# Cross attention on one Trainium2 core: weighted sums in five runs per half instead of seven, and a ring of three buffers for the turned probabilities

## The chip, the cores and the metric

One core of one Trainium2 chip runs the whole program. The metric is device time in microseconds (us), the median of several executions. Beside it stands one execution recorded by the hardware profiler, from which all rows come.

## What is computed

The kernel runs twelve residual blocks one after the other: in each of four layers a cross attention, a self attention and a feed-forward part. The change lies in the four cross attentions. There x has 16 batches of 64 queries, and the context 16 batches of 1601 keys, both of width 256, with 16 heads of 16:

```python
def _L1_xattn_ref(q, k, v, Wq, bq, Wk, bk, Wv, bv, Wo, bo):
    qh = _split_heads(q @ Wq.T + bq)
    kh = _split_heads(k @ Wk.T + bk)
    vh = _split_heads(v @ Wv.T + bv)
    score = jnp.einsum('bhqd,bhkd->bhqk', qh, kh) / jnp.sqrt(jnp.float32(D_K))
    attn = jax.nn.softmax(score, axis=-1)
    out = jnp.einsum('bhqk,bhkd->bhqd', attn, vh)
    ...
    return out @ Wo.T + bo
...
x = x + _L1_xattn_ref(_layernorm(x, axis=-1), ctx_1024, ctx_1024, ...)
```

Layer 0 adds a mask to the scores, layer 2 replaces scores where a mask is 0, and layers 1 and 3 have no mask.

## The kernel before, in words

`cross_attention` works through 32 **halves** per layer: a half is one batch and 8 of its 16 heads (u = 0 to 31, u // 2 the batch). A half holds 4 rows of 128 (two heads by 64 queries) against 1601 keys, and it runs in STEPS = 7 steps, i = 0 to 6, each for two blocks of 128 keys (the last step has one block of 65). The five engines each run a list that is written out by hand, and meet by semaphores. All of them walk over `steps()`. A step of half u does work for several halves at once, on TensorE (`pe()`) in this order:

- **scores** of the next half, chunk i of 400 keys, in steps 0 to 3 only (`scores`, L453): 12 matmuls with 32 rows of contraction, one third for each of three passes, into PSUM banks 0 to 3, one bank per row of heads.
- **turn** of this half (`turn`, L465): 8 transposes of the probabilities (4 in step 6) into banks 4 and 5. It waits in `bank(...)` until the copy of the turn before has emptied them.
- **keys** of the half after the next, chunk i // 2, in even steps (`make_keys`, L481), 6 matmuls into bank 7 in the places that matter here, or **values** of the next batch in odd steps (`make_values`, L495), 12 matmuls into bank 7. In step 6 of odd u there is a further value group of one block, ahead of the keys.
- **weighted** sum (`weighted`, L510): 8 matmuls of the turned probabilities with the values (4 for the last block), each with 32 output columns, into bank 6. Step i weights what step i - 1 turned. Step 0 weights the last group of the half before, and then spreads its denominators (`spread_denominators`, L520), 4 matmuls of the same shape.

On VectorE (`dve()`), a step takes the scores out with their row maxima (`largest`, L617 with a mask and L620 without, four operations for the four banks), then copies the turned probabilities (L575) in steps 4 to 6, takes out values 2, 5 and 6 of a batch (L585), and makes the high and the low part of the keys (`keys_high` L639, `keys_low` L647). In layer 2 only L636 reads the keys' bank, and GpSimd makes the parts. In step 0 VectorE also ends the half before (`outputs`: L659, L662, L664), for which it needs the spread denominators. ScalarE (`act()`) copies the turned probabilities of steps 0 to 3 (L575), makes the high part of key chunks 0 and 1 (L717), takes out the other values (L585), and does the exponentials (L711) from step 4 on. GpSimd splits the context (L784, L786) and makes the diagonals of the denominators (L826).

The turned probabilities lie in `prob_t`, a ring of two groups; `ring(u, i)` says which. `turned_ready` makes a copy wait until the weighting two groups earlier has read its buffer.

From here the text says S0 to S3 for the scores of a step, T0 to T6 for the turns, K for the keys, V for the values, W0 to W6 for the weighted sums (by the group that they weight, not by the step that runs them), and R for the spread denominators. Half A is one with even u, half B the one with odd u behind it. Only half B has the extra value group in step 6.

Of the kernel before, what the change touches and what calls it, by code (L numbers as in the profile page):

```python
# [15 lines left out]
P = 128  # L16
# [264 lines left out]
STEPS = (KT + 1) // 2  # L281
CH = len(KCH)
TURNED, HEADS, UNIT = 4, 6, 7
LAST = HALVES - 1

def cross_attention(k, L, scale, mask=None, wo='Wo', bo='bo'):

# [4 lines left out]
    st = Stage(k)  # L292
# [6 lines left out]
    kept = st.tile("kept", [P, KEYS]) if mask == 'fill' else None  # L299
    vals = [st.tile(f"vals{i}", [P, KT, D]) for i in range(2)]  # L300
    prob = [st.tile(f"prob{i}", [P, ROWS, KEYS]) for i in range(2)]
    prob_t = st.tile("prob_t", [P, 2, 2, 512])
    q_heads = st.tile("q_heads", [P, C, P])
    q_parts = [st.tile(f"q_parts{i}", [P, 2, C, P], F32R) for i in range(2)]
    mx = st.tile("mx", [P, ROWS, CH])
# [57 lines left out]
    def turn_bank(u, i):  # L363

        return 0 if u == LAST and i % 2 else TURNED

    def blocks(i):
        return [x for x in (2 * i, 2 * i + 1) if x < KT]

    def rows_of(x):  # L370
        return min(P, KEYS - x * P)

    def steps():


        for u in range(-2, HALVES):
            for i in range(STEPS):
                chunk = i // 2 if i % 2 == 0 and u + 2 < HALVES else None
                pairs = []
                if u // 2 + 1 < B:  # L380
                    pairs = [i // 2 + 3 * (u % 2)] if i % 2 else [6] if i == 6 and u % 2 else []
                yield u, i, u >= 0, 0 <= u + 1 < HALVES and i < CH, chunk, pairs
# [4 lines left out]
    def values_out(b, n):  # L387

        if values_by_act(n):
            return st.at('v_act', 4 * b + (0, 1, 3, 4).index(n) + 1)  # L390
        return st.at('v_dve', 3 * b + (2, 5, 6).index(n) + 1)

    def turned_out(u, i):

        if u == LAST:
            return st.at('pt_dve' if i % 2 else 'pt_act', (3 if i % 2 else 4) * u + i // 2 + 1)
        return st.at('pt_act', 4 * u + i + 1) if i < 4 else st.at('pt_dve', 3 * u + i - 3)

    def turned_by_act(u, i):
        return i % 2 == 0 if u == LAST else i < 4  # L400

# [4 lines left out]
    def out_tiles(u, i):  # L406

        return [t for t in ([i - 1] if u == LAST - 1 else [i + 5]) if 0 <= t < T - 1 and (u < LAST or i == 1)]

    def ring(u, i):  # L410
        return (u * STEPS + i) % 2

    def sp():
        sp = nc.sync
# [18 lines left out]
    def pe():  # L433
# [7 lines left out]
        def scores(h, i):  # L441
            b, g = h // 2, h % 2
            k0, kw = KCH[i]
            pe.wait_ge(*st.at('k_lo', CH * h + i + 1))
            if i == 0:
                pe.wait_ge(*st.at('q_lo', b + 1))
            for m, (qp, kp) in enumerate(PASSES):
                for r in range(ROWS):
                    if m == 0:
                        bank(r)  # L450
                        free[r] = st.at('s_out', ROWS * (CH * h + i) + r + 1)
                    rows = slice(32 * r, 32 * r + 32)
                    mm = pe.matmul(ps[:, r, 0:kw], q_parts[b % 2][rows, qp, g, :], keys[g][rows, kp, k0:k0 + kw],  # L453
                                   start=(m == 0), stop=(m == 2))
            mm.then_inc(st['s_mm'], 1)

        def turn(u, i):
            if i == 0:
                pe.wait_ge(*st.at('exp', ROWS * (u + 1)))
            for a, x in enumerate(blocks(i)):  # L460
                w = rows_of(x)
                bank(turn_bank(u, i) + a)
                free[turn_bank(u, i) + a] = turned_out(u, i)
                for r in range(ROWS):
                    mm = pe.transpose(ps[0:w, turn_bank(u, i) + a, r * P:(r + 1) * P], prob[u % 2][:, r, x * P:x * P + w],  # L465
                                      cst['ident'][:])
            mm.then_inc(st['t_mm'], 1)

        def make_keys(h, i):
            b, g = h // 2, h % 2  # L470
            k0, kw = KCH[i]
            to = key_bank(h, i)
            bank(to)
            free[to] = keys_out(h, i)
            if h == 0 and i == 0:
                pe.wait_ge(*weights_out(1))
            if g == 0:
                pe.wait_ge(*st.at('ctx_lo', CH * b + i + 1))
            for c in range(C):
                for m, (wp, xp) in enumerate(PASSES):  # L480
                    mm = pe.matmul(ps[:, to, 0:kw], wk[:, wp, c, g * P:(g + 1) * P], ctx[:, xp, c, k0:k0 + kw],  # L481
                                   start=(c == 0 and m == 0), stop=(c == C - 1 and m == 2))
            mm.then_inc(st['k_mm'], 1)

        def make_values(b, n):
            to = value_bank(b, n)
            w = rows_of(blocks(n)[-1])
            if b == 0 and n == 0:
                pe.wait_ge(*weights_out(2))
            bank(to)  # L490
            free[to] = values_out(b, n)
            for a, x in enumerate(blocks(n)):
                for c in range(C):
                    for m, (xp, wp) in enumerate(PASSES):
                        mm = pe.matmul(ps[0:w, to, a * D:(a + 1) * D], ctx[:, xp, c, x * P:x * P + w], wv[:, wp, c, :],  # L495
                                       start=(c == 0 and m == 0), stop=(c == C - 1 and m == 2))
            mm.then_inc(st['v_mm'], 1)

        def weighted(u, i):
            b, g = u // 2, u % 2  # L500
            if i == 0:
                pe.wait_ge(*values_out(b, 4))
                pe.wait_ge(*values_out(b, 6))
                if u:
                    pe.wait_ge(*st.at('both', u))
            pe.wait_ge(*turned_out(u, i))
            for a, x in enumerate(blocks(i)):
                w = rows_of(x)
                for r in range(ROWS):
                    mm = pe.matmul(ps[32 * r:32 * r + 32, HEADS, g * P:(g + 1) * P],  # L510
                                   vals[b % 2][0:w, x, (ROWS * g + r) * 32:(ROWS * g + r + 1) * 32],
                                   prob_t[0:w, ring(u, i), a, r * P:(r + 1) * P], start=(x == 0), stop=(x == KT - 1))
            mm.then_inc(st['pv_mm'], 1)

        def spread_denominators(u):
            pe.wait_ge(*st.at('diag', ROWS * (u + 1)))
            if u:
                pe.wait_ge(*st.at('rmask', u))
            for r in range(ROWS):
                mm = pe.matmul(ps[32 * r:32 * r + 32, HEADS, 2 * P:3 * P], cst['pairblk'][:], diag[:, r, :], start=True,  # L520
                               stop=True)
            mm.then_inc(st['rm_mm'], 1)

        def project_queries(n):
            if n == 0:
                pe.wait_ge(*st.at('Wq', 16))
                pe.wait_ge(*st.at('xnt', T // 2))
            for m in range(C):
                for c in range(C):
                    mm = pe.matmul(ps[:, 2 * n + m, :], wq[:, c, m * P:(m + 1) * P], qt[:, c, n * 512:(n + 1) * 512],  # L530
                                   start=(c == 0), stop=(c == C - 1))
                mm.then_inc(st['q_mm'], 1)
                free[2 * n + m] = st.at('q', C * n + m + 1)
# [13 lines left out]
        for u, i, attend, score, chunk, pairs in steps():  # L547
            if score:
                scores(u + 1, i)
            if attend:  # L550
                turn(u, i)
            if 6 in pairs:
                make_values(u // 2 + 1, 6)
            if chunk is not None:
                make_keys(u + 2, chunk)
            elif pairs:
                make_values(u // 2 + 1, pairs[0])
            if u == -2 and i in (2, 4):
                project_queries(i // 2 - 1)
            if u >= LAST - 1:  # L560
                for t in out_tiles(u, i):
                    project_out(t)
            if attend and i:
                weighted(u, i - 1)
            if u >= 1 and i == 0:
                weighted(u - 1, STEPS - 1)
                spread_denominators(u - 1)
        weighted(LAST, STEPS - 1)
        spread_denominators(LAST)
        project_out(T - 1)  # L570
# [6 lines left out]
    def turned_ready(engine, u, i):  # L577
        n = u * STEPS + i
        engine.wait_ge(*st.at('t_mm', n + 1))
        if n >= 2:  # L580
            engine.wait_ge(*st.at('pv_mm', n - 1))

    def values_copy(copy, sem, b, n):
        w, nb = rows_of(blocks(n)[-1]), len(blocks(n))
# [249 lines left out]

    sp()
    pe()
    dve()
    act()
    pool()
    n = HALVES  # L840
# [1146 lines left out]
```

## Time and profile before

| | us |
|---|---|
| median of 3 executions | 4708.85 (4707.19 to 4713.68) |
| the profiled execution, its own time | 4705.95 |
| its span, first to last instruction | 4704.6 |
| mean granted TensorE clock | 0.938 of full speed |
| TensorE matmuls busy, whole span | 4263.6 (91%) |
| VectorE busy | 3130.7 (67%) |
| ScalarE busy | 2186.8 (46%) |
| GpSimd busy | 1512.5 (32%) |

The four cross attentions begin at about 38, 1098, 2180 and 3616 us of the span and take about 750 us each, two thirds of the whole. In the profile PE is TensorE's matmuls, PEld its weight loads, DVE VectorE, ACT ScalarE, POOL GpSimd. An fp32 matmul of the weighted sums has two records, so that "x16" there is 8 instructions; a turn's "x8" is 8 instructions. A matmul's end in the profile is modelled, so places in time are best read at the weight loads.

### The profile page before, as it was taken

To read this page: it belongs to the slowest core of one execution; us is meant where nothing else is said; L and a number is where in the kernel's file an instruction comes from. 1 tells how busy PE (TensorE), PEld (TensorE's weight loads), DVE (VectorE), ACT (ScalarE), POOL (GpSimd) and SP (SyncE) were. 2 spreads that over 40 slices of the span, in tenths; PEclk is the share of its full clock that TensorE was granted. 3 is DMA by queue.
4 is the path that set the end of the run, shared out by engine and by line. 5 is a ranking of instruction groups with operands and counts; after the bars stand their busy time and mean duration, and the time that the engine had idled before them with its cause. 6 is when DMAs were issued, how large, how long until landed. Compare 5 with 4: busy or idle time off the path is not lost. (4 is left out here: it accounts for less than half of the span.)

```text
span 4704.6 us, 101125 instructions
## 1 busy us (share of the span) xinstructions
PE 4263.6 (91%) x41976; PEld 3386.7 (72%) x41976; DVE 3130.7 (67%) x7563; ACT 2186.8 (46%) x2988; POOL 1512.5 (32%) x1592
## 2 busy tenths in 40 slices
PE   8999999648999999688999999469999999999689
PEld 6888886427888886366888887248887888888368
DVE  5777776776777776715777777464444777777644
ACT  4555554244555554223555555223433555555345
POOL 3434341203332331404656563232211332332221
PEclk9999999769999999867999999769999999999889
DMA  3212120002111110002111110011101111110011
GB/s 85 61 47 64 48 61 16 21 0 60 33 40 33 40 37 22 1 18 69 49 58 51 58 51 23 15 37 37 54 19 46 33 40 33 40 37 16 15 46 37
DMA packets 113944, 181.96 MB, mean 39 GB/s; under 512 B 11104, under 2 KB 102480, under 8 KB 113488
## 3 DMA queue, kind: packets, MB, share of 16 engines
q1 hardware_dynamic: 113488, 175.49, 12.6%
q8 instruction: 334, 5.47, 0.5%
q14 instruction: 122, 1.00, 0.1%
HBM read 174.42 MB, written 1.05 MB: 37 GB/s over the span
## 5 line engine op out<-in xcount | busy, mean ns | idle before, releaser
L575 ACT COPY prob_t<-ps 128x1024 f32<-128x1024 f32 x512 | 518.7, 1013 | 1230.4 <-PE ps L465 1230.4
L465 PE MATMUL ps<-c_ident,prob 128*128 128x128 f32 (+1 forms) x6656 | 924.3, 280 | 9.9 <-ACT prob L711 9.9
L465 PEld LDWEIGHTS ps<-c_ident,prob 128*128 128x128 f32 (+1 forms) x6656 | 712.0, 141 | 221.1 <-issue 208.2
L711 ACT ACTIVATE prob<-prob,nmx 128x1601 f32<-128x1601 f32 x512 | 829.9, 1627 | 1.2 <-DVE nmx L626 1.1
L495 PE MATMUL ps<-wv,ctx 128*128 128x256 f32 x4992 | 706.4, 290 | 3.1 <-DVE vals L585 3.1
L481 PE MATMUL ps<-ctx,wk 128*128 128x400 f32 (+1 forms) x3072 | 687.6, 359 | 7.8 <-POOL ctx L773 3.8
L495 PEld LDWEIGHTS ps<-wv,ctx 128*128 128x128 f32 x4992 | 619.3, 186 | 16.6 <-DVE vals L585 4.0
L575 DVE COPY prob_t<-ps 128x1024 f32<-128x1024 f32 (+1 forms) x384 | 403.5, 1051 | 326.3 <-PE ps L465 326.3
L617 DVE CUSTOM_DVE_ANT_0 prob<-ps,mk 128x400 f32<-128x400 f32 (+2 forms) x1024 | 526.4, 570 | 97.1 <-PE ps L453 93.3
L620 DVE TENSOR_SCALAR_CACHE_REDUCE prob<-ps 128x400 f32<-128x400 f32 (+2 forms) x1024 | 526.7, 571 | 67.9 <-PE ps L453 60.8
L510 PE MATMUL ps<-prob_t,vals 128*32 128x128 f32 x13312 | 548.8, 279 | 0.6 <-DVE prob_t L575 0.6
L481 PEld LDWEIGHTS ps<-ctx,wk 128*128 128x128 f32 x3072 | 535.5, 191 | 11.9 <-issue 5.3
L453 PE MATMUL ps<-keys,q_parts 32*128 32x400 f32 (+1 forms) x6144 | 486.3, 379 | 4.6
L784 POOL CAST ctx<-raw_ctx 128x804 fp32r<-128x804 f32 x240 | 204.7, 853 | 815.3 <-PE ps L481 815.3
L510 PEld LDWEIGHTS ps<-prob_t,vals 128*32 128x32 f32 x13312 | 308.8, 109 | 189.2 <-issue 121.2
L786 POOL TENSOR_TENSOR ctx<-raw_ctx,ctx 128x804 fp32r<-128x804 f32 x240 | 402.9, 1679 | 19.3
L453 PEld LDWEIGHTS ps<-keys,q_parts 32*128 32x128 f32 x6144 | 281.3, 184 | 140.8 <-issue 99.6
L1723 PE MATMUL ps<-x_parts,parts_w 128*114 128x512 f32 (+1 forms) x1536 | 364.4, 398 | 2.5 <-ACT hid_f L1788 1.4
L647 DVE SCALAR_TENSOR_TENSOR keys<-ps,cols,keys 128x400 fp32r<-128x400 f32 (+2 forms) x384 | 243.3, 634 | 168.4 <-ACT keys L717 161.3
L826 POOL TENSOR_TENSOR diag<-c_ident,rden 128x128 f32<-128x128 f32 x512 | 188.6, 400 | 492.3 <-DVE rden L654 492.3
L1723 PEld LDWEIGHTS ps<-x_parts,parts_w 128*114 128x114 f32 (+1 forms) x1536 | 277.1, 181 | 85.9 <-ACT hid_f L1788 4.0
L1735 PEld LDWEIGHTS ps<-parts_wout,hid 114*128 114x128 f32 (+1 forms) x1920 | 227.4, 188 | 1.5
(308 smaller groups left out, 4789.4 us busy)
## 6 DMA issues: line engine op xcount, KB each, us to landing
raw_ctx<-in_ctx_t SPq DMA_DIRECT2D x120, 400.0 KB, 3.2
raw_ctx<-in_ctx_t SPq DMA_DIRECT2D x60, 402.0 KB, 5.0
raw_ctx<-in_ctx_t SPq DMA_DIRECT2D x60, 399.0 KB, 3.2
mk<-in_mask_f SPq DMA_DIRECT2D x32, 400.2 KB, 5.4
mk<-in_mask_i SPq DMA_DIRECT2D x16, 800.5 KB, 4.3
raw_w<-in_L_ffn_w SPq DMA_DIRECT2D x16, 684.0 KB
raw_wout<-in_L_ffn_wout SPq DMA_DIRECT2D x8, 684.0 KB
raw_w<-in_L_ffn_w SPq DMA_DIRECT2D x8, 512.0 KB
```

What stands on the lines that cost most here:

```text
L453: mm = pe.matmul(ps[:, r, 0:kw], q_parts[b % 2][rows, qp, g, :], keys[g][rows, kp, k0:k0 + kw], start=(m == 0), stop=(m == 2))
L465: mm = pe.transpose(ps[0:w, turn_bank(u, i) + a, r * P:(r + 1) * P], prob[u % 2][:, r, x * P:x * P + w], cst['ident'][:])
L481: mm = pe.matmul(ps[:, to, 0:kw], wk[:, wp, c, g * P:(g + 1) * P], ctx[:, xp, c, k0:k0 + kw], start=(c == 0 and m == 0), stop=(c == C - 1 ...
L495: mm = pe.matmul(ps[0:w, to, a * D:(a + 1) * D], ctx[:, xp, c, x * P:x * P + w], wv[:, wp, c, :], start=(c == 0 and m == 0), stop=(c == C ...
L510: mm = pe.matmul(ps[32 * r:32 * r + 32, HEADS, g * P:(g + 1) * P], vals[b % 2][0:w, x, (ROWS * g + r) * 32:(ROWS * g + r + 1) * 32], prob_ ...
L575: copy(prob_t[0:w, ring(u, i), 0:nb, :], ps[0:w, turn_bank(u, i):turn_bank(u, i) + nb, :]).then_inc(st[sem], 1)
L617: v.tensor_tensor_reduce(o, ps[:, r, 0:vw], mk[b % 2][:, k0:k0 + vw], 1.0, NEG, ALU.add, ALU.max, mx[:, r, i:i + 1]).then_inc(st['s_out'], 1)
L620: v.tensor_scalar(o, ps[:, r, 0:vw], 0.0, NEG, ALU.add, ALU.max, accum_out=mx[:, r, i:i + 1]).then_inc(st['s_out'], 1)
L647: v.scalar_tensor_tensor(keys[g][:, 1, k0:k0 + vw], ps[:, key_bank(h, i), 0:vw], k.col(name + 'bk')[:, g:g + 1], keys[g][:, 0, k0:k0 + vw] ...
L711: a.activation(prob[h % 2][:, r, :], prob[h % 2][:, r, :], ACT.Exp, bias=nmx[:, r:r + 1], accum_out=den[h % 2][:, r:r + 1]).then_inc(st['e ...
L786: p.tensor_tensor(ctx[:, 1, :, columns(i)], raw, ctx[:, 0, :, columns(i)].bitcast(F32), ALU.subtract).then_inc(st['ctx_lo'], 1)
L1723: mm = pe.matmul(ps[0:FT, bank, :], parts[w][p][:, a, c, m * FT:(m + 1) * FT], x_parts[:, b, c, toks], start=(c == 0 and q == 0), stop=(c ...
```

## The change

The weighted sums are no longer run one per step. A table says which groups step i weights: step 1 takes W0, step 2 W1, step 3 W2, step 4 none, step 5 W3 and W4 together, step 6 none, and step 0 of the next half W5, W6 and R. The ring grows to three groups, and a copy waits for the weighting three groups earlier.

```diff
@@ -282,6 +282,7 @@
 LAST = HALVES - 1
+WEIGHTED_AT = {1: (0,), 2: (1,), 3: (2,), 5: (3, 4)}
@@ -299,7 +300,7 @@
-    prob_t = st.tile("prob_t", [P, 2, 2, 512])
+    prob_t = st.tile("prob_t", [P, 3, 2, 512])
@@ -408,7 +409,7 @@
     def ring(u, i):
-        return (u * STEPS + i) % 2
+        return (u * STEPS + i) % 3
@@ -560,11 +561,14 @@
-            if attend and i:
-                weighted(u, i - 1)
+            if attend:
+                for x in WEIGHTED_AT.get(i, ()):
+                    weighted(u, x)
             if u >= 1 and i == 0:
+                weighted(u - 1, STEPS - 2)
                 weighted(u - 1, STEPS - 1)
                 spread_denominators(u - 1)
+        weighted(LAST, STEPS - 2)
         weighted(LAST, STEPS - 1)
         spread_denominators(LAST)
@@ -577,8 +581,8 @@
         engine.wait_ge(*st.at('t_mm', n + 1))
-        if n >= 2:
-            engine.wait_ge(*st.at('pv_mm', n - 1))
+        if n >= 3:
+            engine.wait_ge(*st.at('pv_mm', n - 2))
```

What it moves on TensorE is seen best in the order of its instructions. Only this engine's order changes. First the steps 4 to 6 of a half B, from its T4 to the scores of the next half, before:

```order
L465 MATMUL ps<-c_ident,prob_14 128x128 x8
L481 MATMUL ps<-ctx,wk 128x400 x6
L510 MATMUL ps<-prob_t,vals_11 32x128 x8
L465 MATMUL ps<-c_ident,prob_14 128x128 x8
L495 MATMUL ps<-wv,ctx 128x256 x12
L510 MATMUL ps<-prob_t,vals_11 32x128 x8
L465 MATMUL ps<-c_ident,prob_14 65x128 x4
L495 MATMUL ps<-wv,ctx 65x256 x6
L481 MATMUL ps<-ctx,wk 128x400 x6
L510 MATMUL ps<-prob_t,vals_11 32x128 x8
L453 MATMUL ps<-keys_7,q_parts_18 128x402 x12
```

and the same place in the changed kernel, whose lines lie one further down:

```order
L466 MATMUL ps<-c_ident,prob_14 128x128 x8
L482 MATMUL ps<-ctx,wk 128x400 x6
L466 MATMUL ps<-c_ident,prob_14 128x128 x8
L496 MATMUL ps<-wv,ctx 128x256 x12
L511 MATMUL ps<-prob_t,vals_11 32x128 x16
L466 MATMUL ps<-c_ident,prob_14 65x128 x4
L496 MATMUL ps<-wv,ctx 65x256 x6
L482 MATMUL ps<-ctx,wk 128x400 x6
L454 MATMUL ps<-keys_7,q_parts_18 128x402 x12
```

The weighted sum between the keys and T5 is gone, the one behind the values has twice the length, and the scores now follow the keys directly. (A half A has the same rows without the one of 65x256, the extra value group.)

The second place is step 0 of the next half, its T0 to the scores of step 1, before:

```order
L465 MATMUL ps<-c_ident,prob_13 128x128 x8
L481 MATMUL ps<-ctx,wk 128x402 x6
L510 MATMUL ps<-prob_t,vals_11 32x128 x4
L520 MATMUL ps<-diag,c_pairblk 32x128 x4
L453 MATMUL ps<-keys_7,q_parts_18 128x400 x12
```

and in the changed kernel:

```order
L466 MATMUL ps<-c_ident,prob_13 128x128 x8
L482 MATMUL ps<-ctx,wk 128x402 x6
L511 MATMUL ps<-prob_t,vals_11 32x128 x12
L521 MATMUL ps<-diag,c_pairblk 32x128 x4
L454 MATMUL ps<-keys_7,q_parts_18 128x400 x12
```

W5's 8 matmuls have come here, ahead of W6 and R, and behind the keys of step 0.

## Rows read from the trace of the kernel before

**Rows 1.** The page: its span, and the busy time of each engine.

```profile
span 4704.6 us, 101125 instructions
PE 4263.6 (91%) x41976; PEld 3386.7 (72%) x41976; DVE 3130.7 (67%) x7563; ACT 2186.8 (46%) x2988; POOL 1512.5 (32%) x1592
```

**Rows 2.** Busy time by stretch: cross attention of layers 0 and 2, all engines.

```profile
38.00:788.00 750.00, 744.99 (x8781) 608.35 (x8779) 558.20 (x1529) 418.98 (x539) 284.01 (x294) 1.00 0.18 49
...
2180.00:2940.00 760.00, 754.78 (x8789) 614.23 (x8787) 562.44 (x1496) 382.09 (x477) 426.07 (x531) 1.00 0.15 48
```

**Rows 3.** Timeline, weight loads, layer 0: start us, us, instruction, [idle before <-releaser].

```profile
399.86 0.85 PEld L465 LDWEIGHTS ps<-c_ident,prob 128*128 128x128 f32 x8 [0.20 <-issue]
400.68 1.04 PEld L481 LDWEIGHTS ps<-ctx,wk 128*128 128x128 f32 x6
401.99 0.38 PEld L510 LDWEIGHTS ps<-prob_t,vals 128*32 128x32 f32 x16 [0.27 <-issue]
402.57 0.85 PEld L465 LDWEIGHTS ps<-c_ident,prob 128*128 128x128 f32 x8 [0.20 <-issue]
403.48 1.47 PEld L495 LDWEIGHTS ps<-wv,ctx 128*128 128x128 f32 x12
405.09 0.38 PEld L510 LDWEIGHTS ps<-prob_t,vals 128*32 128x32 f32 x16
405.66 0.41 PEld L465 LDWEIGHTS ps<-c_ident,prob 128*65 128x65 f32 x4 [0.20 <-issue]
406.05 1.02 PEld L481 LDWEIGHTS ps<-ctx,wk 128*128 128x128 f32 x6
407.33 0.38 PEld L510 LDWEIGHTS ps<-prob_t,vals 128*32 128x32 f32 x16 [0.26 <-DVE prob_t L575]
407.91 0.49 PEld L453 LDWEIGHTS ps<-keys,q_parts 32*128 32x128 f32 x12 [0.20 <-issue]
...
409.48 1.04 PEld L481 LDWEIGHTS ps<-ctx,wk 128*128 128x128 f32 x6
...
410.92 0.24 PEld L520 LDWEIGHTS ps<-diag,c_pairblk 128*32 128x32 f32 x8
411.36 0.48 PEld L453 LDWEIGHTS ps<-keys,q_parts 32*128 32x128 f32 x12 [0.20 <-issue]
...
415.12 0.51 PEld L453 LDWEIGHTS ps<-keys,q_parts 32*128 32x128 f32 x3 [0.20 <-issue]
415.95 0.48 PEld L453 LDWEIGHTS ps<-keys,q_parts 32*128 32x128 f32 x9 [0.31 <-DVE mx L617]
```

**Rows 4.** Timeline, VectorE, layer 0, the stretch of rows 3.

```profile
400.99 1.22 DVE L575 COPY prob_t<-ps 128x1024 f32<-128x1024 f32 x1 [1.66 <-PE ps L465]
...
402.80 0.63 DVE L647 SCALAR_TENSOR_TENSOR keys<-ps,cols,keys 128x400 fp32r<-128x400 f32 x1
...
408.11 0.63 DVE L647 SCALAR_TENSOR_TENSOR keys<-ps,cols,keys 128x399 fp32r<-128x399 f32 x1
...
411.52 0.64 DVE L647 SCALAR_TENSOR_TENSOR keys<-ps,cols,keys 128x402 fp32r<-128x402 f32 x1 [0.67 <-ACT keys L717]
412.07 0.28 DVE L659 COPY rmask<-ps 128x128 f32<-128x128 f32 x1
```

**Rows 5.** Timeline, weight loads: 12 weighted matmuls in one run, at layer 0's end.

```profile
787.06 0.67 PEld L510 LDWEIGHTS ps<-prob_t,vals 128*32 128x32 f32 x24 [0.40 <-DVE prob_t L575]
787.71 0.24 PEld L520 LDWEIGHTS ps<-diag,c_pairblk 128*32 128x32 f32 x8
```

**Rows 6.** Timeline, weight loads: keys followed by scores, near layer 0's start.

```profile
55.53 1.04 PEld L481 LDWEIGHTS ps<-ctx,wk 128*128 128x128 f32 x6
56.84 0.49 PEld L453 LDWEIGHTS ps<-keys,q_parts 32*128 32x128 f32 x12 [0.26 <-issue]
```

**Rows 7.** Timeline, VectorE, layer 2, a half A: its one key operation.

```profile
2502.33 0.62 DVE L636 SCALAR_TENSOR_TENSOR kf<-ps,cols,kept 128x400 f32<-128x400 f32 x1
```

**Rows 8.** Timeline, weight loads, layer 2, the same half: its T5.

```profile
2502.75 0.86 PEld L465 LDWEIGHTS ps<-c_ident,prob 128*128 128x128 f32 x8 [0.20 <-issue]
```

## The prediction

> **What bounds the kernel now.** The page comes first: matmuls are busy 91% of the span, VectorE 67% [rows 1]. The busy time by stretch is sharper: in the 750 us of layer 0's cross attention TensorE's matmuls are busy 745 us, VectorE 558, ScalarE 419 and GpSimd 284, at the full granted clock of 1.00 [rows 2]. TensorE's queue sets the time there, so the timeline of its weight loads is the view that counts. Two things are to be seen in it. Each time the shape of the tiles changes, the loads sit idle: 0.27 us ahead of W3, 0.20 behind it, 0.26 and 0.20 around W5, always put down to "issue" [rows 3]. That is time the change could win. The second is a wait on another engine, which hides there as a gap in start times: V starts at 403.48, though T5 ahead of it began 402.57 and a turn is otherwise followed after 0.82 (T4 at 399.86, K at 400.68) [rows 3]. V is 0.09 us late because VectorE's L647 left the same bank at 402.80 + 0.63 = 403.43 [rows 4]. So step 4 is already tied to VectorE, with no room. The opposite place is S2 of half B, which begins at 415.12 and gets its last nine loads only at 415.95 [rows 3]: 0.8 us of slack in which TensorE may be late for nothing.
>
> **What the change does on TensorE.** Matmuls are neither added nor removed; 8 of W3 move from step 4 to step 5, 8 of W5 from step 6 to the next step 0. No DMA moves, and no other engine's list changes.
>
> A moved group costs, inside a longer run, what its matmuls stream: 12 in one run took 787.71 - 787.06 = 0.65 us to the next instruction's start [rows 5], 0.054 each, 0.43 for 8. The bounds are 0.38, the span of eight's loads, and 0.58, a whole short run with its drain behind it (407.33 to 407.91) [rows 3]; I take 0.43, since rows 5 are that very case.
>
> Step 4: K to T5 took 402.57 - 400.68 = 1.89; with nothing between, K's loads last 1.04 and the next begins as they end, so 1.0. That frees 0.89, of which 0.43 is work that comes back, and 0.46 are two drains.
> Step 6: K to S0 took 407.91 - 406.05 = 1.86. Keys followed directly by scores took 56.84 - 55.53 = 1.31 [rows 6], since that is a change of shape too. That frees 0.55, 0.43 of which comes back, so 0.12 to 0.13 net.
> By TensorE alone a half would shorten by 0.46 + 0.13 = 0.59 us.
>
> **What is late next.** W3 stood between K and T5, and covered VectorE's work on T4. T5 must wait for the copy of T4, which ends at 400.99 + 1.22 = 402.21 [rows 4]; with 0.05 for the semaphore (403.43 to 403.48) T5 starts at 402.26, not at the 401.7 it could. After its 0.82 it would be V's turn at 403.08, but the bank is VectorE's until 403.43: VectorE still has to copy T4 and make two key parts in that order, none of which the change speeds up. So V starts at 403.48 as before. The whole gain of step 4 is lost in two waits, and the 0.43 of W3 is then added behind V: T6 moves from 405.66 to 406.09, K to 406.48, S0 to 407.79, 0.12 earlier than before. The ring of three permits later weighting, but gives nothing by itself: the copies' idle is put down to the turn (L465) and not to a weighting [rows 4].
>
> Step 0 of half B: T0 and K come with S0, 0.12 earlier (K 409.36). The bank is free for it: VectorE's L647 ends at 408.74 + 0.43 = 409.17. VectorE's next key part waits for ScalarE, which waits for K, so it goes from 411.52 to 411.40. R is later, by 0.43 - 0.12 = 0.31, from 410.92 to 411.23, and about 0.5 until its results are there, 411.74; L659 then would start at 411.95 [rows 4]. It just fits. So from here VectorE is 0.12 early and TensorE 0.31 late. S2 waits for VectorE, with 0.8 us of slack: half B goes on 0.12 early. Its steps 4 to 6 repeat the account, another 0.13 early. In step 0 of the next half A TensorE again gets 0.43 of W5; there is no wait like that at 415.95 in a half A, so it is paid. Per pair of halves: 0.43 - 0.13 - 0.13 = **+0.17 us**.
>
> Layer 2 differs: bank 7 is free after one operation, 2502.33 + 0.62 = 2502.95 [rows 7], so only T5's wait for its copy remains. T5 goes from 2502.75 [rows 8] to about 2502.46, V with it, T6 0.14 later, S0 0.42 earlier, and step 0 gives the 0.43 back. In its half B VectorE's mask work and row maxima come behind the last key operation, which is 0.14 later. I take +0.12 per pair, between 0 and 0.2.
>
> Sum: of 32 halves the first and the last stand apart, so 15 pairs; 15 in each of three layers at 0.17 is 7.7, 15 at 0.12 is 1.8. The last half of a layer has no keys or values, and loses about 0.3 of drains, against 0.1 in the half before: 4 times -0.2, -0.8. Total **+8.7 us**. On the profiled execution's 4705.95 that is 4714.7; the median of the runs shown stands 2.9 above it, so 4717.5.
>
> **Rivals.**
> 1. The drains come off the time. Rows 3 speak for it: two idle stretches vanish with each run taken out. 0.59 us in 30 halves of 4 layers is 71 us, 4638. Against it stands the V that starts 0.05 after L647 [rows 3, 4]: that start can't move unless VectorE does. It would take a T5 and a V that don't wait for VectorE. The Trainium skill names the drain, in "TensorEngine Tiling (Array Packing)", Key Properties: "Changing tiling mode (not just tile) drains the TensorE". Rows 3 agree with it, by 0.26 ahead of a run and 0.20 behind it; followed alone, it gives this rival's 4638 and not my sum. I give it 0.10.
> 2. Slower, clearly: a group inside a joined run costs a whole short run, 0.58 and not 0.43. The place is the run of 16 behind V and the run of W5, W6 and R. Then each pair pays 0.15 in A's step 0, in A's step 5 and in B's step 5, and in B's step 0 R's results come at 411.89, still hidden. That is +0.62 per pair, about 60 pairs, 37 us less 0.8, 4745. It decides from about 0.44 per group on. Rows 5 speak against it, but with VectorE's and ScalarE's traffic different there. Half of it would give 4731. A chance of 0.15.
> 3. Nothing happens in sum: the lost wait and the drains even out, because V's wait is a little shorter than taken or the slack in half A a little larger. 4709, 0.05.
>
> The forecast itself keeps 0.70. Its own range is 4706 to 4729: 0.1 us more or less in a pair is 6 us, and if R's results come late for L659, each 0.1 us costs 4.5 us, as 45 halves B in the three layers lose it.
>
> **How the numbers follow.** Two tenths of a percent, 9.4 us, is about what a measurement of this kernel can tell from no change, so the bounds are 4699.4 and 4718.3. My 4717.5 lies just inside, so the forecast's 0.70 splits: 0.42 within, 0.28 above. Faster: rival 1, 0.10. Same: 0.42 and rival 3, 0.47. Slower: 0.28 and rival 2, 0.43. The range 4702 to 4738 takes in the forecast, rival 3 and the lower half of rival 2; left out are rival 1 and the rest of rival 2, under 0.2.
>
> **What would show it.** In the profile after: fewer idle stretches from "issue" ahead of L465 and the weighted sums; a new wait of TensorE for VectorE's L575 copy at T5, 0.3 to 0.6 us, and one for VectorE's L647 ahead of V, some 0.4 us, in every half of layers 0, 1 and 3; V to T6 longer by 0.43; K to S0 1.31; W5 to S1 longer by 0.43. The distance from T4 to V should stay at 3.62. If it shrinks, rival 1 is at work; if V to T6 grows by 0.58, rival 2. If half B lengthens rather than half A, R was late for VectorE. The forecast is wrong as a whole if half A and half B together get shorter than before.

## The result, and the profile after

The changed kernel takes 4715.58 us (median of 22 executions, 4708.97 to 4722.97) against 4707.53 (22 executions, 4702.51 to 4713.68) for the kernel before, timed with it. The ratio is 1.0016, with a 95% interval of 1.0010 to 1.0023: slower by 8 us, clear of the noise and just inside the 0.2% (9.4 us) that the prediction took as the bound of no change. The forecast was 4717.5, +0.18% of its own median.

The page of the changed kernel, its span and busy times:

```profile
span 4721.7 us, 101121 instructions
PE 4242.8 (90%) x41976; PEld 3398.0 (72%) x41976; DVE 3113.6 (66%) x7563; ACT 2182.8 (46%) x2988; POOL 1514.0 (32%) x1592
```

This execution took 4722.97 us, 17 more than the profiled one of before; it is the slowest of its 22. Only a part of the 17 is the change. The change touches the distance from the first R to the last R of a layer, 31 halves. In layer 0 of the changed kernel these are (the view of the second ends at 790 us and so counts 7 of its 8)

```profile
85.14 0.24 PEld L521 LDWEIGHTS ps<-diag,c_pairblk 128*32 128x32 f32 x8
...
789.87 0.23 PEld L521 LDWEIGHTS ps<-diag,c_pairblk 128*32 128x32 f32 x7
```

704.73 us apart, against 701.92 before, where the first one is

```profile
85.79 0.24 PEld L520 LDWEIGHTS ps<-diag,c_pairblk 128*32 128x32 f32 x8
```

and the last at 787.71 [rows 5]. Read in the same way, layer 1 went from 702.64 to 705.24, layer 3 from 702.37 to 705.31 and layer 2 from 712.20 to 711.53. The four together are +7.7 us, where the medians say +8. The other 9 us of this pair of executions lie in the stages between, where both programs are the same.

The timeline of the weight loads in the changed kernel, from T4 of a half A through step 0 of half B to its S2, answers to [rows 3]:

```profile
400.14 0.85 PEld L466 LDWEIGHTS ps<-c_ident,prob 128*128 128x128 f32 x8 [0.20 <-issue]
400.96 1.04 PEld L482 LDWEIGHTS ps<-ctx,wk 128*128 128x128 f32 x6
402.55 0.85 PEld L466 LDWEIGHTS ps<-c_ident,prob 128*128 128x128 f32 x8 [0.55 <-DVE prob_t L579]
403.76 1.48 PEld L496 LDWEIGHTS ps<-wv,ctx 128*128 128x128 f32 x12 [0.36 <-DVE keys L651]
405.37 0.81 PEld L511 LDWEIGHTS ps<-prob_t,vals 128*32 128x32 f32 x32
406.38 0.41 PEld L466 LDWEIGHTS ps<-c_ident,prob 128*65 128x65 f32 x4 [0.20 <-issue]
406.77 1.03 PEld L482 LDWEIGHTS ps<-ctx,wk 128*128 128x128 f32 x6
408.06 0.48 PEld L454 LDWEIGHTS ps<-keys,q_parts 32*128 32x128 f32 x12 [0.26 <-issue]
...
410.92 0.60 PEld L511 LDWEIGHTS ps<-prob_t,vals 128*32 128x32 f32 x24 [0.26 <-issue]
411.50 0.24 PEld L521 LDWEIGHTS ps<-diag,c_pairblk 128*32 128x32 f32 x8
411.94 0.48 PEld L454 LDWEIGHTS ps<-keys,q_parts 32*128 32x128 f32 x12 [0.20 <-issue]
...
415.70 0.19 PEld L454 LDWEIGHTS ps<-keys,q_parts 32*128 32x128 f32 x3 [0.20 <-issue]
416.09 0.47 PEld L454 LDWEIGHTS ps<-keys,q_parts 32*128 32x128 f32 x9 [0.19 <-DVE mx L621]
```

Counted from T4 (400.14; before, 399.86): T5 comes after 2.41 us (before 2.71) and now waits for the copy of T4; V comes after 3.62, exactly as before, and now waits for VectorE's low key part; V to T6 has grown from 2.18 to 2.62 (403.76 to 406.38), +0.44; K to S0 is 1.29 (before 1.86). In S2 the rest of the loads come 0.39 us after the first three (before 0.83): part of half B's slack is now used.

How often, the waits of the weight loads say (columns: us in total, times, longest):

```profile
PEld ps L466 <- issue: 183.8, 760, 0.5
PEld ps L466 <- DVE prob_t L579: 69.7, 124, 0.9
PEld ps L496 <- DVE keys L651: 33.5, 96, 0.4
```

T5 waits 0.56 us in nearly every half of all four layers, V 0.35 in the halves of the three layers without the fill mask. In place of that the idle put down to "issue" ahead of the turns fell from 208.2 to 183.8 us, and ahead of the weighted sums from 121.2 to 72.2.

### The profile page after: what moved, and what is told of

It is laid out like the page before. It is cut to its first block and busy times, and to the rows that moved or that the text cites. A ratio compares the mean times of both kernels' runs of the same rounds, so it can differ in the third digit from the quotient of the medians.

```text
span 4721.7 us, 101121 instructions
## 1 busy us (share of the span) xinstructions
PE 4242.8 (90%) x41976; PEld 3398.0 (72%) x41976; DVE 3113.6 (66%) x7563; ACT 2182.8 (46%) x2988; POOL 1514.0 (32%) x1592
## 5 line engine op out<-in xcount | busy, mean ns | idle before, releaser
L466 PEld LDWEIGHTS ps<-c_ident,prob 128*128 128x128 f32 (+1 forms) x6656 | 711.6, 141 | 266.3 <-issue 183.8
L511 PE MATMUL ps<-prob_t,vals 128*32 128x128 f32 x13312 | 497.3, 277 | 0.4
L454 PE MATMUL ps<-keys,q_parts 32*128 32x400 f32 (+1 forms) x6144 | 468.9, 379 | 3.0
L511 PEld LDWEIGHTS ps<-prob_t,vals 128*32 128x32 f32 x13312 | 324.5, 109 | 122.6 <-issue 72.2
L651 DVE SCALAR_TENSOR_TENSOR keys<-ps,cols,keys 128x400 fp32r<-128x400 f32 (+2 forms) x384 | 243.3, 634 | 128.3 <-ACT keys L721 121.2
```

## The experiments

Each was timed against the kernel before on the same chip. To compare them, the distance between the R of one half A and the next, a pair of halves, was read in the middle of each layer; within a layer it repeats to 0.1 us or better, and in one kernel layers 0, 1 and 3 agree to 0.1 us. It is 46.45 us before and 46.62 after in layer 0, 47.10 and 47.07 in layer 2.

**Ring of three alone.** The change without its new order:

```diff
-WEIGHTED_AT = {1: (0,), 2: (1,), 3: (2,), 5: (3, 4)}
+WEIGHTED_AT = {1: (0,), 2: (1,), 3: (2,), 4: (3,), 5: (4,), 6: (5,)}
-                weighted(u - 1, STEPS - 2)
-        weighted(LAST, STEPS - 2)
```

> Only the ring of three, with the weighted sums in seven runs as before. My account (the copies wait for turns, never for a weighting): no change, 4708 within 3 us, and TensorE's timeline as before. If instead the ring of two held copies up, it would be faster by more than 5 us.

Measured: 4705.34 against 4705.74, ratio 0.9999 (0.9990 to 1.0008), and 46.46 us per pair. The ring does nothing by itself; in this kernel it is only the licence to weight later.

**W5 alone into step 0.**

```diff
-WEIGHTED_AT = {1: (0,), 2: (1,), 3: (2,), 5: (3, 4)}
+WEIGHTED_AT = {1: (0,), 2: (1,), 3: (2,), 4: (3,), 5: (4,)}
```

> Ring of three; W3 stays in step 4, only W5 goes from step 6 into the next step 0. My account: K to S0 shrinks from 1.87 to 1.31 us in every half (-0.55), half B's step 0 absorbs the 0.43 of W5 in its wait for VectorE, half A's pays it: -0.67 us per pair in layers 0, 1 and 3 and -0.2 to -0.4 in layer 2, -35 us in all, 4672. If the drains of a run don't come off (the change's gain and loss come from elsewhere), 4705 to 4710. If R coming later holds VectorE up, half B shortens by less than 0.5 and the total stays above 4685.

Measured: 4671.84 against 4705.74, 0.9931 (0.9917 to 0.9944). A pair takes 45.75 us in layer 0, -0.70, and 46.76 in layer 2, -0.34. So one half of the change is a gain of 34 us, of the size expected.

**W3 alone into step 5.**

```diff
-WEIGHTED_AT = {1: (0,), 2: (1,), 3: (2,), 5: (3, 4)}
+WEIGHTED_AT = {1: (0,), 2: (1,), 3: (2,), 5: (3, 4), 6: (5,)}
-                weighted(u - 1, STEPS - 2)
-        weighted(LAST, STEPS - 2)
```

> Ring of three; only W3 goes from step 4 into the run with W4; W5 stays in step 6. My account: T4 to V stays 3.62 us in layers 0, 1 and 3, V to T6 grows by 0.43 in every half, nothing is won: +0.86 per pair there and +0.28 in layer 2, +43 us in all, 4751. If a joined run really saved its drains (rival 1), faster than 4700.

Measured: 4755.51 against 4705.74, 1.0105 (1.0091 to 1.0119): 50 us slower, where 43 were expected. A pair takes 47.34 in layer 0, +0.89, and 47.38 in layer 2, +0.28. Its weight loads from T4 to T6:

```profile
404.61 0.85 PEld L466 LDWEIGHTS ps<-c_ident,prob 128*128 128x128 f32 x8 [0.20 <-issue]
405.44 1.04 PEld L482 LDWEIGHTS ps<-ctx,wk 128*128 128x128 f32 x6
407.02 0.86 PEld L466 LDWEIGHTS ps<-c_ident,prob 128*128 128x128 f32 x8 [0.54 <-DVE prob_t L577]
408.24 1.49 PEld L496 LDWEIGHTS ps<-wv,ctx 128*128 128x128 f32 x12 [0.35 <-DVE keys L649]
409.86 0.81 PEld L511 LDWEIGHTS ps<-prob_t,vals 128*32 128x32 f32 x32
410.87 0.41 PEld L466 LDWEIGHTS ps<-c_ident,prob 128*65 128x65 f32 x4 [0.20 <-issue]
```

V comes 3.63 us after T4 again. One run fewer, and the kernel is 50 us slower: the drains that vanish are spent waiting, and W3's matmuls are paid behind V. The two halves of the change add up: -0.70 and +0.89 make +0.19 per pair in layer 0, where both together gave +0.17, and -34 and +50 make +16 us where both gave +8, within what two such intervals allow.

**W2 and W3 in step 4, W5 in step 0.** The same number of runs as the change, but the one that vanishes is that of step 3, ahead of T4, where no engine is waited for:

```diff
-WEIGHTED_AT = {1: (0,), 2: (1,), 3: (2,), 5: (3, 4)}
+WEIGHTED_AT = {1: (0,), 2: (1,), 4: (2, 3), 5: (4,)}
```

> Ring of three; W2 moves from step 3 into step 4 ahead of T5, together with W3 (none in step 3), and W5 into the next step 0. The run that vanishes now stands where nothing waits for VectorE: V to T4 loses both drains and W2's 0.43 goes between K and T5, where TensorE waits anyway. My account: -0.47 us per half from that, and what W5 alone gives: about -90 us, 4618. If T4 waits for ScalarE's copy of T3, the first part shrinks: a wait of TensorE for the copy of T3 at T4 would show it, and 4640 or more.

Measured: 4640.02 against 4705.74, 0.9861 (0.9847 to 0.9874); 45.13 us per pair in layer 0. The direction is right and the size is not: 66 us won of 90. The reason named beforehand, a wait for ScalarE's copy, isn't there. What is, the loads show:

```profile
410.04 1.49 PEld L496 LDWEIGHTS ps<-wv,ctx 128*128 128x128 f32 x12
411.47 0.90 PEld L466 LDWEIGHTS ps<-c_ident,prob 128*128 128x128 f32 x8
412.41 1.03 PEld L482 LDWEIGHTS ps<-ctx,wk 128*128 128x128 f32 x6
```

T4 to K takes 0.94 us instead of 0.82, and nothing is named as waited for. In the matmuls' own timeline T4 starts at 411.57 and K at 412.41, 0.84 apart as in any turn that isn't followed by a wait; it is T4's loads that began early, by 0.10. And the run of step 3 had less to give than the one of step 4: no idle is listed ahead of the weighted loads behind V, which start 0.14 after V's end (403.48 + 1.47 = 404.95, then 405.09), where behind K they sit idle for 0.26 [rows 3]. Of the 0.46 expected, 0.14 ahead and 0.20 behind, less the 0.12 by which T4 to K grew, 0.22 is left. The experiment with the banks shows the same early loads between K and T5.

**Free banks.** Between S3 and the next S0, banks 0 to 3 hold nothing once VectorE has read them. T5 was turned into banks 2 and 3, and the values of step 5 put into bank 0:

```diff
     def value_bank(b, n):
         if n == 6:
             return TURNED + 1
+        if b and n in (2, 5):
+            return 0
...
-        return 0 if u == LAST and i % 2 else TURNED
+        return 0 if u == LAST and i % 2 else 2 if i == 5 else TURNED
```

> The changed kernel, with T5 turned into banks 2 and 3 and the values of step 5 into bank 0 (free between S3 and the next S0) instead of banks 4, 5 and 7. Both waits on VectorE in steps 4 and 5 are gone. My account: T4 to V shrinks from 3.62 to 2.64 us in layers 0, 1 and 3 (3.24 to 2.64 in layer 2), everything behind it comes with it: -1.96 us per pair and -1.2 in layer 2, -106 us against the changed kernel, 4609. If the lost gain had another cause than these two banks (drains that are not really saved), 4700 or more.

> The changed kernel with only T5 in banks 2 and 3; the values stay in bank 7. My account: T5 starts 1.0 after K, but V still waits for VectorE's low key part: T4 to V stays 3.62 in layers 0, 1 and 3, nothing won there. In layer 2 V is free earlier: -0.2 per half. In all -7 us against the changed kernel, 4708. If the wait at T5 were the one that costs, 4660.

> The changed kernel with only the values of step 5 in bank 0; T5 still waits for the copy of T4. My account: V starts 0.82 after T5, at T4 + 3.23 and not + 3.62: -0.39 per half in layers 0, 1 and 3, nothing in layer 2, -35 us against the changed kernel, 4680.

| in the changed kernel | us | of the kernel before (95%) | pair, layer 0 | pair, layer 2 |
|---|---|---|---|---|
| as it is | 4715.58 | 1.0016 (1.0010 to 1.0023) | 46.62 | 47.07 |
| T5's banks only | 4703.48 | 0.9988 (0.9980 to 0.9997) | 46.61 | 46.48 |
| V's bank only | 4681.12 | 0.9943 (0.9931 to 0.9956) | 45.84 | 47.03 |
| both | 4630.41 | 0.9833 (0.9820 to 0.9846) | 44.98 | 46.17 |

With T5's banks alone, T5 follows K at once, and V waits for the rest:

```profile
399.88 0.85 PEld L466 LDWEIGHTS ps<-c_ident,prob 128*128 128x128 f32 x8 [0.20 <-issue]
400.71 1.04 PEld L482 LDWEIGHTS ps<-ctx,wk 128*128 128x128 f32 x6
401.74 0.98 PEld L466 LDWEIGHTS ps<-c_ident,prob 128*128 128x128 f32 x8
403.50 1.48 PEld L496 LDWEIGHTS ps<-wv,ctx 128*128 128x128 f32 x12 [0.79 <-DVE keys L651]
```

T4 to V is 3.62 us still: the wait moved from T5 to V and grew from 0.36 to 0.79, and layer 0 won nothing. In layer 2, where V's bank is free earlier, the pair got 0.59 shorter where 0.4 was expected, and the median lies 12 us below the changed kernel's where 7 were. With V's bank alone, V starts 0.83 after the waiting T5:

```profile
419.11 1.03 PEld L484 LDWEIGHTS ps<-ctx,wk 128*128 128x128 f32 x6
420.69 0.86 PEld L468 LDWEIGHTS ps<-c_ident,prob 128*128 128x128 f32 x8 [0.55 <-DVE prob_t L581]
421.52 1.47 PEld L498 LDWEIGHTS ps<-wv,ctx 128*128 128x128 f32 x12
```

That is -0.78 per pair in layer 0, 0.39 per half, as expected, and next to nothing in layer 2. With both, neither wait is left, and the kernel is 85 us faster than the changed one by the medians (86 by the ratios), 20 short of the 106 expected. The loads there:

```profile
410.26 0.86 PEld L468 LDWEIGHTS ps<-c_ident,prob 128*128 128x128 f32 x8 [0.20 <-issue]
411.09 1.03 PEld L484 LDWEIGHTS ps<-ctx,wk 128*128 128x128 f32 x6
412.12 0.98 PEld L468 LDWEIGHTS ps<-c_ident,prob 128*128 128x128 f32 x8
413.06 1.47 PEld L498 LDWEIGHTS ps<-wv,ctx 128*128 128x128 f32 x12
```

T4 to V is 2.80, not 2.64. T5's loads start 1.03 behind K's, but V's follow only 0.94 after them. The timeline of the matmuls of the same kernel tells why:

```profile
411.11 1.34 PE L484 MATMUL ps<-ctx,wk 128*128 128x400 f32 x6
412.30 1.03 PE L468 MATMUL ps<-c_ident,prob 128*128 128x128 f32 x8
413.09 1.65 PE L498 MATMUL ps<-wv,ctx 128*128 128x256 f32 x12
```

T5's first load starts at 412.12 and its first matmul only at 412.30. Between blocks of one shape the first load starts ahead of its own matmul, 0.18 us here. The 1.0 us for K with nothing behind it was read from the loads, and from K's first matmul to T5's it is 1.19. The gain from the run taken out is that much smaller.

**Free banks, W3 and W4 apart.** This measures the worth of a run's two drains by itself, where nothing waits with the run or without it:

```diff
-WEIGHTED_AT = {1: (0,), 2: (1,), 3: (2,), 5: (3, 4)}
+WEIGHTED_AT = {1: (0,), 2: (1,), 3: (2,), 4: (3,), 5: (4,)}
```

on top of the free banks.

> The free banks for T5 and the values of step 5, W3 back in step 4 and W4 alone in step 5, W5 in the next step 0: six runs where the free banks with W3 and W4 together have five, and no wait in steps 4 and 5 in either. The difference is what one run's two drains are worth. By my prediction's 0.46 per half: 0.46 x 120 = 55 us slower than the free banks alone (4630), 4685. By the timeline of the free banks (T4 to V 2.80 us where I had 2.64) only 0.3 or less: 33 us slower, 4663.

Measured: 4666.05 against 4706.60, 0.9917 (0.9903 to 0.9931). To the free banks with the joined run, 4630.41, that is 36 us over 120 halves by the medians and 40 by the ratios, 0.30 to 0.33 us per run. The pair distances say 0.29 (45.56 us in layer 0, 0.58 more than with the joined run).

**W2 and W3 in step 4 alone**, with W5 back in step 6:

```diff
-WEIGHTED_AT = {1: (0,), 2: (1,), 3: (2,), 5: (3, 4)}
+WEIGHTED_AT = {1: (0,), 2: (1,), 4: (2, 3), 5: (4,), 6: (5,)}
-                weighted(u - 1, STEPS - 2)
-        weighted(LAST, STEPS - 2)
```

> Ring of three, W2 joins W3 in step 4, W5 stays in step 6: six runs, and none vanishes where VectorE is waited for. By my prediction's 0.46 per run -0.47 x 120 = -56 us, 4652. By the size seen since (with W5 in step 0 it brought 32 us), 0.27 per half: 4676.

Measured: 4674.83 against 4706.60, 0.9934 (0.9921 to 0.9948), 32 us or 0.26 per half. That is an average of two cases. In layer 2 a pair got 0.42 shorter, 0.21 per half, near the 0.22 above. In layer 0 it got 0.62 shorter, 0.31 per half, because V's own small wait for VectorE went too: T5 to V takes 0.82 there, where it took 0.91 in rows 3. Both halves of the run with W5 in step 0 are now known, 34 and 32, and their sum is its 66.

**Ring of four, four runs.** The free banks, and W4 in the next step 0 as well:

```diff
-WEIGHTED_AT = {1: (0,), 2: (1,), 3: (2,), 5: (3, 4)}
+WEIGHTED_AT = {1: (0,), 2: (1,), 4: (2, 3)}
-    prob_t = st.tile("prob_t", [P, 3, 2, 512])
+    prob_t = st.tile("prob_t", [P, 4, 2, 512])
-        return (u * STEPS + i) % 3
+        return (u * STEPS + i) % 4
+                weighted(u - 1, STEPS - 3)
+        weighted(LAST, STEPS - 3)
-        if n >= 3:
-            engine.wait_ge(*st.at('pv_mm', n - 2))
+        if n >= 4:
+            engine.wait_ge(*st.at('pv_mm', n - 3))
```

> Both bank changes, a ring of four, and four runs per half: W0 in step 1, W1 in step 2, W2 and W3 in step 4, and W4, W5, W6 and R in the next step 0. My account against the free banks alone: steps 3 to 5 shorten by 0.57 us, W4 costs 0.43 in step 0 of a half A, and in a half B makes R late for VectorE's L659 by 0.2 (0.4 in layer 2): -0.48 per pair, -0.28 in layer 2, -26 us, 4583. If step 0 of half B can't take more, it is no better than the free banks alone.

Measured: 4584.93 against 4708.76, 0.9735 (0.9721 to 0.9748): 2.6% faster than the kernel before, and the fastest of all. A pair in layer 0 takes 44.18 us, 0.80 less than with the free banks alone, where 0.48 was expected; the median hit its expectation only because the free banks themselves had come out 20 us above theirs. In a half B the joined run is now W4, W5, W6 and R, and S1's loads follow R by 0.44 as ever:

```profile
415.74 1.03 PEld L513 LDWEIGHTS ps<-prob_t,vals 128*32 128x32 f32 x40 [0.26 <-issue]
416.75 0.24 PEld L523 LDWEIGHTS ps<-diag,c_pairblk 128*32 128x32 f32 x8
417.19 0.49 PEld L456 LDWEIGHTS ps<-keys,q_parts 32*128 32x128 f32 x12 [0.20 <-DVE keys L655]
```

Why it gained more than counted was not tried apart. The loads of layer 0 say where: against the free banks, of W4's 0.43 half B's step 0 lets only 0.07 through (0.2 counted), and the rest of the half is 0.64 us shorter in half B and 0.68 in half A (0.57 counted).

## Why the prediction was right

**The bound, and what is late next.** Right, and the step on which all hangs. V's start is tied to VectorE's L651 (L647 before), and T4 to V stayed at 3.62 us. The two waits were forecast at 0.58 (T5; the row says 0.55) and at some 0.4 (V; 0.36). The experiments with banks show them to be cause and not company: T5's wait taken away alone gives layer 0 nothing, V's alone gives 0.39 per half, both together give 0.82.

**A moved group costs 0.43.** V to T6 grew by 0.44 and from the first of W5 to R it is 0.58, where in the kernel before from W6 to R it was 0.14 (to the 410.92 of rows 3): 0.44 each time.

```profile
410.78 0.16 PEld L510 LDWEIGHTS ps<-prob_t,vals 65*32 65x32 f32 x8 [0.26 <-issue]
```

**K to S0 by 0.55 shorter.** It is 1.29, so 0.57.

**Step 0 of half B absorbs W5.** Right. Per pair in layer 0 the forecast was +0.17 and the trace says +0.17; in layers 1 and 3 the same distance is +0.15 and +0.18. It is also half A that grows, as said: from R to R half B is 0.13 shorter and half A 0.29 longer in layer 0 (forecast 0.13 and 0.30). The experiment with W5 alone, -0.67 forecast and -0.70 measured, and that with W3 alone, +0.86 and +0.89, show that this isn't two errors that cancel in the sum.

The prediction didn't say why half B has this slack and half A has none. In layers 0, 1 and 3 the trace of the kernel before shows it: in half B's step 0 VectorE's small L664 runs beside GpSimd's L786 and takes 1.13 us, in half A's step 0 it runs alone and takes 0.28. VectorE's row maxima come later by the difference, and they are what S2 waits for.

```profile
412.78 1.14 DVE L664 SCALAR_TENSOR_TENSOR XNT<-both,cols 128x64 f32<-128x64 f32 x1
411.93 1.91 POOL L786 TENSOR_TENSOR ctx<-raw_ctx,ctx 128x804 fp32r<-128x804 f32 x1
...
737.92 0.28 DVE L664 SCALAR_TENSOR_TENSOR XNT<-both,cols 128x64 f32<-128x64 f32 x1
```

The last row is from the last but one half B of layer 0, when GpSimd has no more context to split. There S2 isn't held up, and the changed kernel pays for W5: that half got 0.31 longer instead of 0.13 shorter. No experiment took L786 away, but layers 1 and 3 show the same.

**The end of a layer.** Forecast at -0.2 per layer. From the R in step 0 of that half on, the last three distances from R to R changed by +0.31, +0.29 and -0.29 us in layer 0, and by nearly the same in layers 1 and 3. So these three layers grew by 2.81, 2.60 and 2.94 where the prediction's terms make 2.35 each, 1.3 us more in all.

**Layer 2.** The term was mis-sized: "+0.12 per pair" is -0.03, about 2 us of the total. One part came as said: half B's last key operation, 0.14 later by the forecast, holds up VectorE's mask work and row maxima behind it, and from its S0 to the next half A is 0.17 longer (23.95 where it was 23.78). The other part didn't: the prediction let step 0 of half B give back the whole 0.43, and half B is 0.19 shorter (23.12 where it was 23.31). R was late for VectorE there, by 0.41 us, in VectorE's timeline of the changed kernel:

```profile
2519.48 0.29 DVE L663 COPY rmask<-ps 128x128 f32<-128x128 f32 x1 [0.41 <-PE ps L521]
2519.88 0.29 DVE L666 TENSOR_TENSOR both<-ps,rmask 128x128 f32<-128x128 f32 x1
2520.20 0.67 DVE L668 SCALAR_TENSOR_TENSOR XNT<-both,cols 128x64 f32<-128x64 f32 x1
2520.80 0.56 DVE L621 CUSTOM_DVE_ANT_0 prob<-ps,mk 128x400 f32<-128x400 f32 x1
```

But the wait is given back one operation later. L668 took 0.67 us here, and in the kernel before, as L664, it took 1.10 in the same place, beside GpSimd's second key operation:

```profile
2512.31 1.10 DVE L664 SCALAR_TENSOR_TENSOR XNT<-both,cols 128x64 f32<-128x64 f32 x1
2512.28 1.04 POOL L802 TENSOR_TENSOR keys<-kf,keys 128x402 fp32r<-128x402 f32 x1
```

In the changed kernel's GpSimd timeline that operation is

```profile
2519.74 1.05 POOL L806 TENSOR_TENSOR keys<-kf,keys 128x402 fp32r<-128x402 f32 x1
2520.74 0.86 POOL L788 CAST ctx<-raw_ctx 128x804 fp32r<-128x804 f32 x1
```

and L668, begun 0.46 after it, ends 0.08 us after it; L664 began 0.03 after L802 and ended 0.09 after it. VectorE's next row maxima start 4.48 us after the first ones of S0, before 4.45. So VectorE isn't late, and 0.19 of the 0.43 goes into the time for which half B's scores waited for it already.

The sum, +8.7 us forecast and +8 measured, is that near partly by luck: layer 2 came out 2.3 us below its terms and the other three 1.3 above.

**By TensorE alone 0.59 per half.** This step was wrong in size, without touching the sum, since the waits covered it. The 0.46 for the drains around W3 is about 0.30: the runs with the free banks give 36 us for 120 of them, and the run of step 3, behind V, is worth 0.21 where no wait goes with it (layer 2). It was read from starts of weight loads, which run ahead, and the 0.26 ahead of a run was taken for every place. The expectations for two of the experiments were about 20 us too good for the same reasons.

**The rivals.** The first, the drains off the time, fell: 4638 stood against 4716, and with W3 alone moved the drains vanished and the time rose. With the banks free the drains do come off, and that kernel takes 4630; that this is near 4638 is chance in part, since a run is worth 0.30 and not 0.46 and half B's step 0 takes in 0.43 per pair that the rival doesn't count. The rule of the Trainium skill that the prediction quotes for it ("TensorEngine Tiling (Array Packing)", Key Properties), that a change of tiling mode drains TensorE, agrees with these traces: in the middle of the layers the loads sit idle for 0.13 to 0.29 us at each change of shape (0.13 or 0.14 behind V, 0.26 behind K), and between a turn and the keys behind it, of one shape, there is no idle in the kernel before. It doesn't say whether anybody was waiting for TensorE meanwhile. The second, a joined group at a whole run's price, fell with the 0.44. The third, nothing in sum, lay 8 us off, outside the interval.

## What to carry to other kernels

A drain or a gap is worth something only if the next thing can start earlier: follow each block to the semaphore that frees its bank before counting the gap as won. Here the run between K and T5 was free cover for another engine's work, and moving it away left the wait and put its matmuls behind it, while the same edit one step earlier won 0.26 us per half, and a run taken out with two unused banks lent 0.30 to 0.33. When an edit has two parts, time them apart: here -34 and +50 us hid inside a result of +8.

## What the runs showed of the hardware that was not expected

Between blocks of the same tile shape TensorE's first weight load starts ahead of its own first matmul, by an amount that depends on the block before: 0.18 us behind K (loads at 412.12, matmul at 412.30), 0.10 behind V (411.47 and 411.57), 0.03 or less behind a turn. So a distance between loads that has no shape change in it can be shorter than what the array is really held for.

VectorE's small L664 (128x64, two inputs in SBUF) takes 0.28 us alone, as in 57 of its 128 executions in either trace. In the other 71 it meets a two-input GpSimd operation (L786 or L802, one time L219) and ends 0.08 to 0.09 us after that, whenever it began: it takes 1.13, 1.17, 1.10 or 0.67 us, and twice as much as that in one case. So a VectorE operation of 0.28 us can cost a microsecond, and an edit that makes it start 0.4 us later can cost nothing.
